# Three of sixteen columns of the outer products as ScalarE copies, inner pairs last in a batch, and gathers half a batch nearer

## What is computed

```python
e = jnp.stack([tbl_f[ids[:, f]] for f in range(16)], axis=1)      # [2048, 16, 256]
xk, outs = e, []
for i in range(3):
    z = jnp.einsum('bfe,bge->bfge', e, xk).reshape(B, 256, 256)   # all pairs of fields
    z = jnp.einsum('bcl,oc->bol', swapaxes(z, 1, 2), Ws[i]) + bs[i][None, :, None]
    z = jnp.sum(relu(z), axis=-1)                                 # [B, 16]
    outs.append(z)
    xk = jnp.broadcast_to(z[:, :, None], (B, 16, 256))
h = jnp.concatenate([concat(outs), dense_ctx], axis=1)            # [2048, 64]
y = relu(relu(h @ W_top1 + b_top1) @ W_top2 + b_top2) @ W_top3
```

## Time and profile before

| | us |
|---|---|
| median of three runs | 615.01 |
| profiled execution | 614.09 |
| its span, first to last instruction | 612.3 |
| VectorE busy | 577.9 (94%) |
| TensorE busy | 488.1 (80%) |
| GpSimd busy | 458.5 (75%) |
| ScalarE busy | 456.4 (75%) |
| mean granted TensorE clock | 0.922 of 2.4 GHz |

### The profile page before, as it was taken

How to read it: one execution, slowest core, us unless ns; L and a number is a source line. 1 busy time by engine, 2 the same in 40 slices (tenths; PEclk the granted TensorE clock), 3 DMA queues, 4 the chain that set the end, 5 groups by cost and what they waited for, 6 DMA issues and landing times.

```text
span 612.3 us, 10434 instructions
## 1 busy us (share of the span) xinstructions
PE 488.1 (80%) x3932; PEld 191.5 (31%) x3932; DVE 577.9 (94%) x303; ACT 456.4 (75%) x1328; POOL 458.5 (75%) x351
## 2 busy tenths in 40 slices
PE   1589658776869887889898888889977787898947
PEld 0223213332223333234333323334332322333324
DVE  0899996999999999999999999999999999999983
ACT  1243847978796987978897797878888697976785
POOL 6777888888888888888888888888888886433100
PEclk9999989988999897979988797899999799998989
DMA  5333122222221211222222112122222211000000
GB/s 144 95 95 109 56 61 69 70 70 70 60 58 56 61 57 58 70 70 69 70 62 60 56 58 62 55 66 70 70 70 62 58 55 36 1 1 1 2 0 0
DMA packets 14186, 35.39 MB, mean 58 GB/s; under 512 B 5349, under 2 KB 5735, under 8 KB 14122
## 3 DMA queue, kind: packets, MB, share of 16 engines
q0 software_dynamic: 12288, 33.57, 18.7%
q1 hardware_dynamic: 1850, 1.17, 0.8%
HBM read 34.71 MB, written 0.01 MB: 57 GB/s over the span
## 4 chain that ended last, share of the span: by engine, by line
DVE 65%; issue 16%; POOL 9%; ACT 5%; PE 4%; DMA 1%; DVEq 0%; POOLq 0%
DVE prod L285 51%; DVE outer L315 13%; POOL intra L260 5%; POOL x_rows L244 4%; ACT outer L425 3%; PE t_ps L706 1%; DVE intra L297 1%; PE z_ps L612 1%; PE t_ps L581 1%; DMA x_rows<-in_tbl,ids_u 1%; ACT h L457 1%; ACT xt L377 0%; PE t_ps L710 0%; DMA ids_sb<-in_ids 0%; PE turn_ps L684 0%
## 5 line engine op out<-in xcount | busy, mean ns | idle before, releaser
L285 DVE TENSOR_TENSOR prod<-t_ps,xt 128x2048 f32<-128x2048 f32 x192 | 424.8, 2282 | 21.0 <-ACT xt L377 21.0
L244 POOL DMA_INDIRECT x_rows<-in_tbl,ids_u x256 | 246.4, 962 | 74.1 <-issue 71.7
L425 ACT ACTIVATE outer<-outer,bias_sb 128x256 f32<-128x256 f32 x494 | 243.9, 501 | 8.7 <-DVE outer L315 8.7
L612 PE MATMUL z_ps<-prod,w_sb 128*32 128x512 f32 x1536 | 212.5, 676 | 46.9 <-DVE prod L285 45.9
L260 POOL TENSOR_TENSOR intra<-xt 128x1536 f32<-128x1536 f32 (+2 forms) x90 | 211.5, 2385 | 33.7 <-ACT xt L377 33.1
L315 DVE TENSOR_TENSOR outer<-y_ps,z_all 128x2048 f32<-128x2048 f32 (+1 forms) x68 | 143.6, 2157 | 1.9 <-ACT z_all L409 1.2
L377 ACT ACTIVATE xt<-t_ps 128x512 f32<-128x512 f32 x128 | 75.0, 593 | 74.5 <-PE t_ps L581 73.7
L581 PE MATMUL t_ps<-ident,x_rows 128*128 128x128 f32 x512 | 87.6, 302 | 40.4 <-DVE prod L285 22.6
L425 ACT ACTIVATION_READ_ACCUMULATOR outer<-outer,bias_sb 128x1 f32 x494 | 95.9, 194 | 0.0
L612 PEld LDWEIGHTS z_ps<-prod,w_sb 128*32 128x32 f32 x1536 | 48.2, 118 | 148.9 <-issue 133.1
L581 PEld LDWEIGHTS t_ps<-ident,x_rows 128*128 128x128 f32 x512 | 62.0, 155 | 79.3 <-issue 63.0
(11 more groups left out here) (37 smaller groups left out, 155.6 us busy)
## 6 DMA issues: line engine op xcount, KB each, us to landing
x_rows<-in_tbl,ids_u POOLq DMA_INDIRECT x256
w_sb<-in_w SPq DMA_DIRECT2D x1, 512.0 KB, 4.5
ids_sb<-in_ids SPq DMA_DIRECT2D x1, 128.0 KB, 2.1
feat<-in_dense SPq DMA_DIRECT2D x1, 128.0 KB, 3.8
w_sb<-in_w SPq DMA_DIRECT2D x1, 128.0 KB, 4.2
ident<-in_identity SPq DMA_DIRECT2D x1, 64.0 KB, 1.8
w_sb<-in_w0t SPq DMA_DIRECT2D x1, 64.0 KB, 2.1
sel_sb<-in_sel SPq DMA_DIRECT2D x1, 48.0 KB, 1.9
```

Of the source, the lines that this page charges most:

```text
L244: pool.indirect_dma_start(out=x_rows[:, par, f, :], out_offset=None, in_=tables[f], in_offset=bass.IndirectOffsetOnAxis(ap=ids_u[:, NF * b ...
L285: dve.tensor_tensor(prod[:, m % PROD_RING, half, :].rearrange("p (f g s) -> p f g s", f=QF, g=QF), t_ps[:, TBANK[q, half], :, :].unsqueeze ...
L425: act.activation(outer[:, o // OP, o % OP, :], outer[:, o // OP, o % OP, :], ACT.Relu, bias=bias12_sb[:, layer - 1, o:o + 1], accum_out=z_ ...
L612: mm = pe.matmul(z_ps[j * GR:(j + 1) * GR, m % 2, 0:n], w0_sb[:, half, slot, :], src[:, half, j * n:(j + 1) * n], start=(slot == 0 and hal ...
```

## The change

- The last 3 of the 16 columns g of each outer product of batches 0 to 14 (SLICES = 3) are no longer VectorE's. ScalarE writes each as one scaled copy: all 16 o by 16 f of y_ps (256 elements) times the sample's z[g] (slice_outer), six instructions a batch. VectorE's piece covers 13 columns (128x1664) and waits for these copies (semaphore sliced) in place of z0_moved, y_turned and z_ready.
- Parts i0 and i1 are contracted last in a batch and make the fifth bank; u5 alone makes the fourth. Batch 15 keeps the order of before.
- GpSimd issues eight gathers of batch 2 ahead of inner_pairs(1, 0) instead of 16, and all later gathers stand half a batch nearer to their use.
- The cast of the indices goes (they are read as they are), and the indices of batch 0 are loaded by a transfer of their own.
- VectorE's inner pairs of batch 0 are four groups of one quarter each, the first ahead of all products.
- The orders of ScalarE and TensorE are rewritten around this. In the last frame and the tail, z0 of batch 15 is folded ahead of mlp_c, and some moves of the tail change places with sums.

Cut to its core (left out: the last frame, the tail and helpers that follow from it):

```diff
-PARTS = ("u0", "u1", "u2", "sq", "u3", "i0", "u4", "i1", "u5")
-PAIRS = (("u0", "u1"), ("u2", "sq"), ("u3", "u4"), ("i0", "i1"), ("u5",))
+PARTS = ("u0", "u1", "u2", "sq", "u3", "u4", "u5", "i0", "i1")
+PAIRS = (("u0", "u1"), ("u2", "sq"), ("u3", "u4"), ("u5",), ("i0", "i1"))
+LAST_PARTS = ("u0", "u1", "u2", "sq", "u3", "i0", "u4", "i1", "u5")
+LAST_PAIRS = (("u0", "u1"), ("u2", "sq"), ("u3", "u4"), ("i0", "i1"), ("u5",))
-GATHERS_AFTER = {1: 0, 2: 0, 3: 8}
 PIECES = 2
 OP = NF // PIECES
+SLICES = 3
...
-            sp.dma_start(ids_sb[:, :], ids).then_inc(ids_loaded, 16)
+            sp.dma_start(ids_sb[:, 0:NF], ids[:, 0:NF]).then_inc(ids_first, 16)
+            sp.dma_start(ids_sb[:, NF:], ids[:, NF:]).then_inc(ids_loaded, 16)
...
-                field = 2 * pair * QF
                 for d in (1, 2, 3):
                     n = (QF - d) * P
-                    if b > 0:
-                        pool.tensor_tensor(intra[:, pair, :, :, at:at + n], x[:, :, :, 0:n],
-                                           x[:, :, :, d * P:d * P + n], ALU.mult).then_inc(intra_done, 1)
+                    pool.tensor_tensor(intra[:, pair, :, :, at:at + n], x[:, :, :, 0:n],
+                                       x[:, :, :, d * P:d * P + n], ALU.mult).then_inc(intra_done, 1)
                     at += n
-                    gather(b + 2, field, field + GATHERS_AFTER[d])
-                    field += GATHERS_AFTER[d]
-
+
+            pool.wait_ge(ids_first, 16)
+            gather(0, 0, NF)
             pool.wait_ge(ids_loaded, 16)
-            pool.tensor_copy(ids_u[:, :], ids_sb[:, :]).then_inc(ids_cast, 1)
-            pool.wait_ge(ids_cast, 1)
-            for b in range(2):
-                gather(b, 0, NF)
-            for b in range(NB):
-                for pair in range(2):
-                    inner_pairs(b, pair)
+            gather(1, 0, NF)
+            gather(2, 0, NF // 2)
+            for b in range(1, NB):
+                inner_pairs(b, 0)
+                gather(b + 1, NF // 2, NF)
+                inner_pairs(b, 1)
+                gather(b + 2, 0, NF // 2)
...
+                m = NF - slices(b)
+                if m < NF:
+                    dve.wait_ge(sliced, SLICES * (2 * b + layer))
+                else:
+                    if layer == 1:
+                        dve.wait_ge(z0_moved, b + 1)
+                        dve.wait_ge(y_turned, b + 1)
                     dve.wait_ge(z_ready, z_count(b, layer - 1))
-                    if vector_count(b, layer - 1) > 0:
-                        dve.wait_ge(vector_summed, vector_count(b, layer - 1))
-                if layer == 1 and o == 0:
-                    dve.wait_ge(y_turned, b + 1)
+                    dve.wait_ge(vector_summed, vector_count(b, layer - 1))
                 y = y_ps[:, :, :, layer - 1, o:o + n].rearrange("p f c o -> p o (f c)")
                 dve.tensor_tensor(
-                    outer[:, o // OP, o % OP:o % OP + n, :].rearrange("p o (f g) -> p o f g", f=NF),
-                    y.unsqueeze(3).to_broadcast([P, n, NF, NF]),
-                    z_all[:, b % 2, layer - 1, :].unsqueeze(1).unsqueeze(1).to_broadcast([P, n, NF, NF]),
+                    outer[:, o // OP, o % OP:o % OP + n, :].rearrange("p o (f g) -> p o f g", f=NF)[:, :, :, 0:m],
+                    y.unsqueeze(3).to_broadcast([P, n, NF, m]),
+                    z_all[:, b % 2, layer - 1, 0:m].unsqueeze(1).unsqueeze(1).to_broadcast([P, n, NF, m]),
                     ALU.mult).then_inc(outer_done, 1)
...
+                if b == 0:
+                    inner_pairs_first(0)
                 multiply(b, 0)
                 if b == 0:
-                    inner_pairs_first(0)
+                    inner_pairs_first(1)
                 multiply(b, 1)
                 multiply(b, 2)
                 outer_pieces(b - 1, 1)
+                if b == 0:
+                    inner_pairs_first(2)
                 multiply(b, 3)
                 if b == 0:
-                    inner_pairs_first(1)
+                    inner_pairs_first(3)
                 multiply(b, 4)
                 multiply(b, 5)
                 outer_pieces(b - 1, 2)
...
+            def slice_outer(b, layer):
+
+                if not 0 <= b < LAST:
+                    return
+                if layer == 1:
+                    act.wait_ge(z0_moved, b + 1)
+                    act.wait_ge(y_turned, b + 1)
+                if layer == 2 or b > 0:
+                    act.wait_ge(z_ready, z_count(b, layer - 1))
+                y = y_ps[:, :, :, layer - 1, :].rearrange("p f c o -> p o (f c)")
+                out = outer[:, :, :, :].rearrange("p k i (f g) -> p (k i) f g", f=NF)
+                for g in range(NF - SLICES, NF):
+                    act.activation(out[:, :, :, g], y, ACT.Copy,
+                                   scale=z_all[:, b % 2, layer - 1, g:g + 1]).then_inc(sliced, 1)
...
             for frame in range(LAST):
                 b = frame
+                sum_outer(b - 2, 2, OP // 2, OP)
                 copy_tile(b, 2, 1)
-                sum_outer(b - 2, 2, OP // 2, OP)
                 move_zs(b - 1)
                 sum_outer(b - 2, 2, OP, OP + OP // 2)
+                move_z0(b - 1)
                 sum_outer(b - 2, 2, OP + OP // 2, NF)
+                slice_outer(b - 1, 1)
+                move_feat(b - 2)
                 copy_tile(b, 3, 0)
-                move_z0(b - 1)
-                move_feat(b - 2)
                 copy_tile(b, 3, 1)
+                rectify(b, 0)
+                mlp_in(frame, "mlp_a")
+                copy_tile(b + 1, 0, 0)
                 square(b, 0)
-                copy_tile(b + 1, 0, 0)
+                sum_outer(b - 1, 1, 0, OP // 2)
                 square(b, 1)
-                mlp_in(frame, "mlp_a")
-                rectify(b, 0)
                 copy_tile(b + 1, 0, 1)
-                sum_outer(b - 1, 1, 0, OP // 2)
+                mlp_in(frame, "mlp_b")
                 sum_outer(b - 1, 1, OP // 2, OP)
+                sum_outer(b - 1, 1, OP, OP + OP // 2)
+                sum_outer(b - 1, 1, OP + OP // 2, NF)
+                slice_outer(b - 1, 2)
                 rectify(b, 1)
-                mlp_in(frame, "mlp_b")
-                sum_outer(b - 1, 1, OP, OP + OP // 2)
+                rectify(b, 2)
                 copy_tile(b + 1, 1, 0)
-                sum_outer(b - 1, 1, OP + OP // 2, NF)
-                rectify(b, 2)
-                move_yt(b)
                 copy_tile(b + 1, 1, 1)
                 copy_tile(b + 1, 2, 0)
                 sum_outer(b - 1, 2, 0, OP // 2)
+                move_yt(b)
                 rectify(b, 3)
                 rectify(b, 4)
...
             for frame in range(LAST):
                 b = frame
                 transpose_tile(b, 2, 1)
+                turn_y(b - 1)
                 sum_pairs(b - 1, 4)
+                fold_z0(b - 1)
                 contract(b, "u0")
-                fold_z0(b - 1)
                 transpose_tile(b, 3, 0)
-                turn_y(b - 1)
                 contract(b, "u1")
                 form_feat(b - 2)
                 transpose_tile(b, 3, 1)
                 mlp_in(frame, "mlp_a")
                 transpose_tile(b + 1, 0, 0)
+                mlp_in(frame, "mlp_b")
+                transpose_tile(b + 1, 0, 1)
                 contract(b, "u2")
-                transpose_tile(b + 1, 0, 1)
                 contract(b, "sq")
+                transpose_tile(b + 1, 1, 0)
+                form_yt(b)
                 sum_pairs(b, 0)
-                mlp_in(frame, "mlp_b")
                 contract(b, "u3")
-                sum_pairs(b, 1)
-                transpose_tile(b + 1, 1, 0)
-                contract(b, "i0")
                 contract(b, "u4")
-                form_yt(b)
-                sum_pairs(b, 2)
                 transpose_tile(b + 1, 1, 1)
                 transpose_tile(b + 1, 2, 0)
+                sum_pairs(b, 1)
+                contract(b, "u5")
+                contract(b, "i0")
                 contract(b, "i1")
-                contract(b, "u5")
+                sum_pairs(b, 2)
                 sum_pairs(b, 3)
```

109 lines of the change are left out of this document (56 added, 53 removed).

## The result

The changed kernel takes **592.08 us** (median of four runs, 591.91 to 593.83), beside 615.2 (614.21 to 616.88) for the kernel before on the same chip: ratio 0.9628 (0.960 to 0.9656). The profiled execution took 591.95 us. Forecast were 587.3 us and a range of 583 to 601.

What follows compares the result with a forecast made beforehand. VectorE, busy 577.9 of 612.3 us, was taken as the bound. Gains 24.0 + 2.3 + 4.7 + 0.3 = 31.3, minus 0.6 and 3.5, leave 27.2 off 614.1: 586.9, set at 587.3 us towards the median; range 583 to 601.

Steps and rivals of the forecast that it cites:

- Outer pieces: VectorE's outer pieces, batches 0 to 14: 13 columns instead of 16 save 0.400 us on each of 60, 24.0 us.
- Start: Before frame 1: gathers begin 0.9 us sooner and batch 0's inner pairs take 1.4 us less of VectorE's path, 2.3 us.
- GpSimd's order: Early batches: GpSimd multiplies sooner and TensorE asks later for i1, so VectorE's hole of 4.71 us at 92.4 us goes.
- Slips and GpSimd's period: Losses: 3.5 us for TensorE's slow clock (0.25 a batch, 14 batches), 0.6 us for GpSimd's longer batch in the last two.
- The chain of layer 2: ScalarE's work up to layer 2's copies in each batch: done at 28.5 us, wanted at 29.97, 1.4 us to spare.
- Three copies: ScalarE's new column copies for one layer: 0.45 us each, 1.35 us for three, 2.7 a batch.
- the walk: One batch followed in queue order with VectorE as clock: layer 1 has 2.6 us to spare, layer 2 has 1.4.
- Last batch: Batch 15: layer 1's sums start about 0.25 us earlier against outer(14,2), shortening the wait for z0; 0.3 us taken.
- C: Rival: layer 2's chain or a tile copy late in most batches, 17 us lost instead of 3.5, 597 to 605; chance 0.20.
- A: The forecast case: VectorE is the clock, slips of 0 to 0.5 us a batch, 583 to 591 us; chance 0.58.
- B: Rival: VectorE's row of 13 costs more than 13; half the saving lost (12 us) gives 595 to 599; chance 0.13.

Runs made afterwards that it cites:

- late loads: Changed kernel with the perceptrons' loads (0.75 MB) held on SyncE's queue until the first gather has landed: 697.42 us, beside 698.35 unedited.
- the moves back: Changed kernel with ScalarE's last tail moves put behind the sums again, as in the kernel before: 699.95 us, beside 698.35 unedited.
- the second look: Changed kernel unedited, run again on chips where the kernel before had a median of 724.94 us: 698.35 us.

## Why the prediction was right, and where it was not

It named the bound, the sign, and a range that held the time; the time was 4.8 us too low. The terms as measured add up to the span: 24.0 + 1.1 + 4.7 + 0.3 - 5.4 - 2.2 = 22.5 us, beside 22.4. Against the profiled execution (586.9 forecast, 591.95 measured), by its own steps:

- **Outer pieces, 24.0 us: right.** 1880 ns as computed.
- **Start, 2.3 us: 1.1.** The half on the inner pairs held: the next groups are 1.8 us each (22.06 to 23.86), three on the path. The half on the gathers failed: issued 0.6 us sooner (2.93 for 3.54), the first tile was transposed no sooner (12.23 for 11.96). The step took the landing for a fixed time behind the issue; the late loads show that the transfers beside it hold it back. Frame 1 began at 49.49 instead of 48.3: 1.2 us.
- **GpSimd's order, 4.7 us: right** as a size, by the changed kernel's unbroken row at 92 us; which of the two moves (gathers, i1 behind u5) closed the hole is not shown. The first multiplication stood at 54.52 (55.6 forecast), and GpSimd waited, 4.37 and 5.15 us, only behind 520 us.
- **Slips and GpSimd's period, 4.1 us: 5.4** (0.53 at 56.69, 0.23 among the products behind 455.98, 1.48, 1.42, 1.78), 1.3 us more; VectorE never waited for GpSimd's work in the last batches, for which 0.6 was set. The chain of layer 2 was indeed the one without room: 1.4 us to spare was forecast, and the frames without a product in four steps had 0.63 to 1.66. Two things were missed. Three copies take 1.43 us start to start, 0.48 each (1.35 forecast, and 0.40 to 0.5 each as the sign of it), but the end of the last, for which VectorE waits, comes 1.65 us behind the first start. And the walk was made in a frame without a product in four steps. The slip was put on TensorE's clock and spread over 14 batches; it came from a fixed piece of work in three frames, which the trace before already shows (278.70, above). The Trainium skill (Vector Engine (DVE) Microarchitecture Reference, Measured stream behaviour on trn2) had warned of written elements on their own, for VectorE: by its 1.7 to 2.5 ns the estimate was 1.7 to 2.3 us for three. On ScalarE the kind of cost is there and is smaller: 1.64 us to the end of the third, of which the steps are 0.43.
- **Last batch, 0.3 us: right up to z0, wrong behind it.** From outer(14,2) to the first piece behind z0 it took 8.02 us (555.18 to 563.20), 9.14 before (578.64 to 587.78); 0.8 are its shorter pieces and 0.3 the order. From there to the end the sum held 24.5 us as before; it took 26.7. By the rows 1.3 is that product, at the lower granted clock (8.26 us beside 6.98 before for the same instructions), and 0.9 its later start behind the piece, of which the moved steps are 0.3. The other 0.6 goes with the wait of the last half (1.24 us with the moves back, 0.63 before); its cause stays open. A moved tail was costed at nothing without its own walk, and how much of the clock's part another execution would show is open: on the other chip the product took 7.25.

1.2 + 1.3 + 2.2 make 4.7 of the 5.0 us; 0.3 lies outside the span (2.05 us, 1.79 before). All three errors point the same way, so the time did not come right by luck. C's mechanism was right in kind, in three frames instead of most, at about a quarter of its size (4.7 of 17 us); A was the case that happened. The weights of the range add up to 0.81 (0.58, 0.13 and half of 0.20), not 0.83.

B's price for a lone word, 5 us, did not come: 1880 ns is 2280 less 384 elements at 1.04 ns each. It was an application of the Trainium skill (Vector Engine (DVE) Microarchitecture Reference, Measured stream behaviour on trn2) that the page does not state. The page gives the full rate to runs of at least two adjacent words and measured the surcharge on elements that hop each time; it has no row for a run of odd length. A row of 13 is one run of adjacent words, and the trace agrees with the full rate for it.

## What to carry to other kernels

Work moved from the bound engine to one with slack is worth its full price only while the receiver's tightest chain has room: walk that chain in the worst frame of the cycle, with the rare pieces of work in it, not in a typical one. Price a copy by its write pattern, and what waits for it by the copy's end, not by the start of the next instruction. Before a first load is issued earlier, look at what is transferred beside it.

## What was not expected of the hardware

- **A write in steps of 64 bytes made ScalarE's copy of 256 elements 0.21 us longer** (683 beside 472 ns), and took 0.11 us of ScalarE's time (three copies 1.41 beside 1.08 us); reading PSUM in steps of 128 bytes cost nothing.
- **Gathers are held back by setup loads**: 0.75 MB of loads on another queue delayed the first tile by 1.6 to 2.7 us.
- **Engines stood still for whole stretches with nothing to wait for.** The same program took 592 us on one chip and 698 on another. TensorE in the second look at the changed kernel:

```profile
43.01 0.37 PE L615 MATMUL t_ps<-ident,x_rows 128*128 128x128 f32 x1 [1.08 <-issue]
45.81 0.37 PE L615 MATMUL t_ps<-ident,x_rows 128*128 128x128 f32 x1 [2.43 <-issue]
48.61 0.37 PE L615 MATMUL t_ps<-ident,x_rows 128*128 128x128 f32 x1 [2.43 <-issue]
```

One matmul comes every 2.80 us, and nothing in the profile releases it; at first the four transposes of such a tile took 0.60 to 1.1 us together. That the instructions themselves came late is the reading of this document, not shown. The amount of instruction transfers is the same on both (0.51 MB on one queue, 0.15 on the other). It showed on both chips of the experiments, with the kernel before too (722 to 730 us). The cause was not found.
